# Key pieces in six places and an earlier mask in the first layer, pairs of heads in the second layer's attention

## The chip, the cores and the metric

One Trainium2 chip, one core of it. The time is the device time of one execution in microseconds (us), from the first to the last instruction of the program with what lies around it. Lower is better.

## What is computed

Two layers, each of cross attention to a long context, a mixing or attention block and a feed-forward block, with layer norms and residual sums. The work of all six blocks runs in one program. The two blocks that the change touches, with the shapes of this case (2 sequences of 256 tokens, 256 features, a context of 4096):

```python
# first layer, cross attention: 16 heads of 16
q = proj(layernorm(x), Wq, bq); k = proj(ctx, Wk, bk); v = proj(ctx, Wv, bv)
energy = einsum('bhqd,bhkd->bhqk', q, k) / sqrt(16)
energy = where(mask == 0, -1e9, energy)
x = x + softmax(energy) @ v @ Wo.T + bo

# second layer, attention: 16 heads of 64, heads 0-7 causal, heads 8-15 not
q, k = rope(h @ Wq), rope(h @ Wk); v = h @ Wv        # h = layernorm(x)
out_ar   = attend(q[:, :8], k[:, :8], v[:, :8], causal)
out_diff = attend(q[:, 8:], k[:, 8:], v[:, 8:], 0)    # softmax(q k^T / 8 + mask) v
x = x + concat(out_ar, out_diff) @ Wo
```

All is float32 at the interfaces. No key is masked in the inputs, and the kernel finds this out while it runs.

## The kernel before

**Engines and order.** The program is written by hand for each engine: one list of instructions for SP (DMA issues), ScalarE (`act`), VectorE (`dve`), TensorE (`pe`) and GpSimd (`pool`). Each list runs in its order; what ties them together are semaphores that are waited for by value. So the order of two instructions of one engine is that of the source, and one that waits holds up all behind it.

**First layer, up to the first exponentials.** The context of 4096 positions is cut in 8 chunks of 512 (`NCH`), each loaded as 512 KB into one of six slots (`SLOTS`). For each chunk `project_keys` makes two pieces of keys (128 of the 256 features each, four matmul records of 512 columns a piece) and `project_values` two halves of the values (eight records of 256 columns a half). Results go through a ring of three PSUM banks, which ScalarE empties (`copy_keys`, lines 692 and 693; `copy_values`, line 698). Keys and queries are kept as three bfloat16 parts that add up to the float32 value: ScalarE writes the high part and a float32 copy (`K32`, three buffers), VectorE subtracts and casts the middle part (`split_keys`, lines 975 and 977; `split_queries`, lines 961 to 968), and GpSimd subtracts the low part (`low_part`, line 607). A finished piece (`KPT`, three places, number of the piece modulo 3) is stored to DRAM (`store_k`, line 432) and read back in another arrangement as a stack of 96 rows (`load_stack`, six DMAs a quarter, line 440; `QST` for the queries, line 469). A place can be written again when its store has landed.

Meanwhile the mask (int32, four loads of 1 MB on ScalarE's queue, line 661) is turned into bfloat16 on VectorE in eight parts (`mask_part`, line 984), ScalarE sums each part (`sum_mask`, line 683), TensorE adds over partitions (line 1654), VectorE makes a flag (lines 1079 and 1081), and TensorE reads it and branches into `attend(True)` or `attend(False)`; in the latter no matmul adds the mask. `BRANCH` chunks are projected ahead of the branch. In `attend`, what is left of keys and values is interleaved with `scores`, 32 units of 128 queries by 1024 keys (two matmul records of 96 rows, line 1528), each followed by its row maximum on VectorE (`row_tops`, line 991). `LAG` says how many chunks the values stand behind the keys, `UNITS_AT` how many units go with each chunk. After that `turn_max` brings the maxima of the group into the stack, and the long loop over 8 groups of 4 heads starts, in which TensorE makes turned scores (line 1557), ScalarE takes exponentials (line 715) and TensorE weighs the values (line 1575).

**SP's list around it.** Stores of pieces, then, by chunk, the loads of the query stack, of the key stacks' quarters, and of context chunks 6 and 7 into the slots of chunks 0 and 1 when their values are made (line 445).

**Second layer's attention.** After rotation (`f_roped`), queries and keys are turned on TensorE and copied by ScalarE (line 886) so that even heads lie in partitions 0 to 63 and odd heads in 64 to 127. There are 32 units n of one sequence and head, 16 pairs. For each n: `head_scores` (two matmuls, four records, line 1921) into one of four PSUM banks; `row_maxima` on VectorE (for causal heads with the mask added and written to a buffer `PM`, line 1376; else a plain maximum, line 1381; then a negated, scaled copy, line 1383); `head_exps` on ScalarE (line 895); `scale_exps` on VectorE (a reciprocal, line 1389, and two multiplications of 128 rows of queries each, line 1393); `turn_weights` on TensorE (three or four transposes, line 1935, into bank 2 or 3); a copy of these by ScalarE (line 915); and for each pair `weigh_heads` on TensorE (eight records, the two heads to the two halves of the output partitions, line 1952) and `copy_contexts` on VectorE (line 1401). TensorE's loop takes scores of n + 3, turning of n, and after every odd n the weighing of the pair before. The values are projected ahead of the loop (line 1889).

## Time and profile before

| | us |
|---|---|
| median of 3 runs | 1050.47 |
| lowest and highest | 1048.58, 1052.31 |
| profiled execution | 1047.13 |
| its span, first to last instruction | 1045.3 |

| engine | busy us in the span | share |
|---|---|---|
| TensorE (PE) | 916.5 | 88% |
| VectorE (DVE) | 601.9 | 58% |
| ScalarE (ACT) | 487.4 | 47% |
| GpSimd (POOL) | 78.2 | 7% |

The mean granted TensorE clock over the span is 0.951 of full speed. How to read the rows below: times are in us from the span's start unless marked ns. PE is TensorE's matmuls and PEld its weight loads, which overlap; SPq and ACTq are DMA issues of these engines; L12 is line 12 of the kernel. A float32 matmul shows as two records. The chain of waits follows the work that ended last back to the start: at each step to what released it, or to the instruction before it on its engine; "issue" there is time in which the engine waited for nothing that the profile shows.

### The profile page before, as it was taken

The page shows a single profiled execution, that of the slowest core. Times are in us where ns is not written, and L with a number is a line of the kernel's source. Part 1 is how long each engine was busy: PE and PEld are TensorE (multiplying, and loading weights), DVE is VectorE, ACT ScalarE, POOL GpSimd, SP SyncE. Part 2 cuts the span into 40 slices and gives each one's busy share as a digit, 9 for nine tenths or more (in the row PEclk, how much of TensorE's full clock was granted, in tenths as well). Part 3 has the DMA queues.
Part 4 walks back from the last instruction along what each step waited for, and adds up shares of the span by engine and source line. Part 5 has one row for each costly group of instructions (what it writes and reads, how often), then busy time and mean ns, then how long its engine had stood idle before and what let it go on. Part 6 is the DMA issues. An engine that isn't in the chain of part 4 may idle for free.

```text
span 1045.3 us, 14987 instructions
## 1 busy us (share of the span) xinstructions
PE 916.5 (88%) x5913; PEld 527.1 (50%) x5914; DVE 601.9 (58%) x1064; ACT 487.4 (47%) x955; POOL 78.2 (7%) x87
## 2 busy tenths in 40 slices
PE   6379799999999999999988995059999989999878
PEld 2246444444555555555445543034755854566656
DVE  3647777777874458888443836953233127288240
ACT  1623366777764567777884411322220210677201
POOL 2312011111000000000002000300000007000000
PEclk9979899999999999999998998669999989999979
DMA  9845733454322212226028006032625350000000
GB/s 357 220 90 158 250 104 104 139 151 132 87 69 65 61 32 67 74 74 195 15 103 296 1 1 241 0 149 93 241 81 211 112 161 0 1 1 1 1 0 21
DMA packets 65555, 108.67 MB, mean 104 GB/s; under 512 B 6854, under 2 KB 40390, under 8 KB 63302
## 3 DMA queue, kind: packets, MB, share of 16 engines
q1 hardware_dynamic: 63276, 100.35, 30.3%
q10 hardware_dynamic: 2208, 7.34, 1.8%
q8 instruction: 49, 0.80, 0.3%
q14 instruction: 22, 0.18, 0.1%
HBM read 93.77 MB, written 13.89 MB: 103 GB/s over the span
## 4 chain that ended last, share of the span: by engine, by line
PE 79%; DVE 9%; ACT 6%; issue 3%; DMA 2%; SPq 0%; POOL 0%; ACTq 0%; DVEq 0%
PE psum L1575 12%; PE psum L1557 10%; PE psum L1528 10%; PE psum L1512 5%; PE psum L1860 5%; PE psum L1831 5%; PE psum L1502 5%; PE psum L1684 4%; PE psum L1889 4%; PE psum L1697 4%; PE psum L1921 3%; ACT arena L715 2%; PE psum L1935 2%; DVE arena L991 1%; PE psum L2021 1%
## 5 line engine op out<-in xcount | busy, mean ns | idle before, releaser
L991 DVE TENSOR_REDUCE arena<-psum 128x1 f32<-128x1024 f32 x256 | 301.7, 1219 | 121.2 <-PE psum L1528 121.1
L715 ACT ACTIVATE arena<-psum 128x512 f32<-128x512 f32 x512 | 264.7, 604 | 63.6 <-PE psum L1557 62.5
L1557 PE MATMUL psum<-arena 99*128 99x256 bf16 x1024 | 161.3, 275 | 8.4 <-ACT arena L715 4.8
L1528 PE MATMUL psum<-arena 96*128 96x512 bf16 x512 | 152.9, 382 | 6.5 <-DVE arena L991 5.5
L1575 PE MATMUL psum<-arena 128*32 128x256 f32 x2048 | 136.8, 385 | 0.0
L1557 PEld LDWEIGHTS psum<-arena 99*128 99x128 bf16 x1024 | 80.4, 98 | 107.1 <-ACT arena L715 50.6
L1575 PEld LDWEIGHTS psum<-arena 128*32 128x32 f32 x2048 | 53.5, 109 | 75.4 <-ACT arena L715 36.9
L1502 PE MATMUL psum<-arena 128*128 128x512 f32 x128 | 64.3, 630 | 24.1 <-DMA arena<-wkT 9.0
L1512 PE MATMUL psum<-arena 128*128 128x256 f32 x256 | 62.9, 389 | 1.3 <-ACT arena L693 1.3
L1528 PEld LDWEIGHTS psum<-arena 96*128 96x128 bf16 x512 | 49.4, 99 | 25.9 <-DVE arena L991 12.9
L607 POOL TENSOR_TENSOR arena<-arena 128x512 bf16<-128x512 f32 x34 | 40.8, 1199 | 213.4 <-DVE arena L977 206.7
L1512 PEld LDWEIGHTS psum<-arena 128*128 128x128 f32 x256 | 47.8, 192 | 16.7 <-issue 9.6
L1860 PE MATMUL psum<-arena 128*128 128x256 f32 x256 | 55.9, 379 | 0.0
L1831 PE MATMUL psum<-arena 128*128 128x512 f32 x128 | 55.5, 593 | 0.0
L692 ACT ACTIVATE arena<-psum,arena 128x512 bf16<-128x512 f32 x32 | 22.0, 686 | 67.0 <-PE psum L1502 50.3
L1860 PEld LDWEIGHTS psum<-arena 128*128 128x128 f32 x256 | 48.3, 190 | 6.4
L1502 PEld LDWEIGHTS psum<-arena 128*128 128x128 f32 x128 | 24.4, 200 | 49.7 <-issue 39.2
L1684 PE MATMUL psum<-arena 128*128 128x512 f32 (+1 forms) x112 | 44.1, 551 | 3.3 <-ACT arena L781 0.9
L698 ACT ACTIVATE arena<-psum 128x512 f32<-128x512 f32 x32 | 19.1, 597 | 59.7 <-PE psum L1512 59.7
L877 ACT ACTIVATE arena<-psum 128x512 f32<-128x512 f32 x16 | 9.6, 597 | 78.5 <-PE psum L1847 78.5
L1889 PE MATMUL psum<-arena 128*128 128x512 f32 x96 | 43.2, 610 | 0.7 <-ACT arena L779 0.7
L1303 DVE CUSTOM_DVE_ANT_0 arena<-psum,arena 128x512 f32<-128x512 f32 x32 | 22.1, 692 | 32.9 <-PE psum L1831 30.7
(234 smaller groups left out, 989.0 us busy)
## 6 DMA issues: line engine op xcount, KB each, us to landing
arena<-kparts SPq DMA_DIRECT2D x192, 128.0 KB, 3.1
kparts<-arena SPq DMA_DIRECT2D x32, 384.0 KB, 3.4
arena<-ctxT SPq DMA_DIRECT2D x18, 512.0 KB, 5.1
arena<-ctxT SPq DMA_DIRECT2D x2, 4096.0 KB, 12.9
arena<-ctx SPq DMA_DIRECT2D x2, 4096.0 KB, 14.3
arena<-mask SPq DMA_DIRECT2D x8, 1024.0 KB, 6.8
arena<-mask ACTq DMA_DIRECT2D x4, 1024.0 KB, 12.2
arena<-w1e SPq DMA_DIRECT2D x2, 2048.0 KB, 10.2
```

The lines of the kernel that those rows point to most:

```text
L715: nc.scalar.activation(PR[step % 4][:, pair * CH:(pair + 1) * CH], ring_bank(slot), ACT.Exp)\
L991: nc.vector.tensor_reduce(MX[g % 2][:, col:col + 1], unit_banks(n).rearrange("p b n -> p (b n)"), AX.X, ALU.max).then_inc(s_maxed, 1)
L1502: last = nc.tensor.matmul(ring_bank(slot), WK[:, k, f * P:(f + 1) * P], CTX[n % SLOTS][:, k, :], start=(k == 0), stop=(k == CT - 1))
L1512: last = nc.tensor.matmul(ring_bank(slot)[:, v * 256:(v + 1) * 256], CTX[n % SLOTS][:, k, (2 * i + v) * P:(2 * i + v + 1) * P], WV[:, k, : ...
L1528: last = nc.tensor.matmul(out, q, KST[g % 2][0:ROWS, j, at], start=True, stop=not masked, skip_group_check=True)
L1557: last = nc.tensor.matmul(ring_heads(slot)[:, u, :], KST[gg % 2][0:KROWS, j, kc * P:(kc + 1) * P], QST[0:KROWS, G * g + j, b * S:(b + 1) * S],
L1575: last = nc.tensor.matmul(PV[32 * j:32 * (j + 1), :], V_flat[:, at:at + 32], PR[step % 4][:, j * S:(j + 1) * S], start=(kc == 0), stop=(kc ...
L1684: last = nc.tensor.matmul(out, weights[:, k, m * P:m * P + width], xs[k], start=(k == 0), stop=(k == n - 1))
L1697: last = nc.tensor.matmul(out, lhs[k], weights[:, k, :], start=(k == 0 and not biased), stop=(k == n - 1), skip_group_check=biased)
L1831: last = nc.tensor.matmul(psum[:, n % 4, :], QC[:, c, w * P:(w + 1) * P], CTXT[w // 2][:, c, n * 512:(n + 1) * 512], start=(c == 0), stop= ...
L1860: last = nc.tensor.matmul(psum[:, 6, 0:256], PT1[:, k * P:(k + 1) * P], CTXK[w // 2][:, k, :], start=(k == 0), stop=(k == KC - 1))
L1889: last = nc.tensor.matmul(psum[:, bank, :], HTF[:, c, i * P:(i + 1) * P], WQKV[which][:, c, half * HALF:(half + 1) * HALF], start=(c == 0) ...
```

## The change

What it does, in the first layer:

- `KPT` has six places (`PLACES`) up to the last piece of the first sequence and three after it. ScalarE no longer waits for the store three pieces back but for that six pieces back, and besides for the low part three pieces back (the float32 buffers stay three). `piece_number`, `place` and `turn_at` do the counting; the queries' pieces come after two chunks (`EARLY = 2`).
- Masks are loaded after chunks 0 and 1 (of which 1 comes behind masks 0 and 1), the other chunks after all of them. VectorE makes mask parts 0 to 3 after chunk 0 and 4 to 7 after chunk 1, then splits the queries, then waits for the count. ScalarE sums four parts after the keys of chunk 1 and four after those of chunk 2, in place.
- TensorE projects chunk 1 ahead of the queries and chunk 2 behind them, then branches: `BRANCH` 3 instead of 4. `LAG` is 4 instead of 3, so no values are made ahead of the branch; `UNITS_AT` gives 4 units to each of steps 4 to 11, where it was 4 to each of 4 to 9 and 8 to step 10. In `attend` the wait for the query stack stands ahead of the first unit, and each half step has keys, values, two units. The loads of context 6 and 7 stand one chunk later on SP, context 6 behind the second stack.
- The copy of the turned x and the first splits change order on VectorE; a few small loads share semaphores.

In the second layer's attention:

- `head_scores` takes a pair: for each half of the queries the even head and then the odd head. TensorE's loop runs over pairs: scores of the pair two ahead, turning of both heads, weighing of the pair before.
- The factor -1/8 is in ScalarE's copy of the turned queries, so the maximum becomes a minimum and the negated copy is gone.
- `scale_exps` multiplies the second 128 queries on VectorE and GpSimd the first 128.
- Even heads' turned weights are copied by VectorE (`copy_weights`, bank 2), odd ones by ScalarE (bank 3). The values' projection uses four banks instead of five.

```diff
-LAG = 3
-BRANCH = 4
+LAG = 4
+BRANCH = 3
+EARLY = 2
+PLACES = 6
 AHEAD = 6
 RAMP = 5
-UNITS_AT = {4: 4, 5: 4, 6: 4, 7: 4, 8: 4, 9: 4, 10: 8}
+UNITS_AT = {4: 4, 5: 4, 6: 4, 7: 4, 8: 4, 9: 4, 10: 4, 11: 4}
...
-        KPT = [b16(45584 + 768 * i, 1536).rearrange("p (r n) -> p r n", r=3) for i in range(3)]
+        KPT = [b16(at, 1536).rearrange("p (r n) -> p r n", r=3) for at in (45584, 46352, 47120, 41488, 42256, 43024)]
...
         def piece_number(b, c, f):
 
-            return f if b + c == 0 else CT + 2 * NCH * b + 2 * c + f
+            return 2 * NCH * b + 2 * c + f + (CT if b or c >= EARLY else 0)
 
         def query_piece(f):
-            return CT + f
+            return 2 * EARLY + f
+
+        def place(r):
+
+            first = CT + 2 * NCH
+            return r % PLACES if r < first else (r - first) % 3
+
+        def turn_at(r):
+
+            return sum(place(n) == place(r) for n in range(r + 1))
...
+            def chunks_stored(first):
+                for c in (first, first + 1):
+                    for f in range(CT):
+                        stored(piece_number(0, c, f))
+
+            for c in range(EARLY):
+                for f in range(CT):
+                    store_k(0, c, f)
             for f in range(CT):
                 r = query_piece(f)
                 sp.wait_ge(k_low, r + 1)
+                sp.dma_start(qparts[:, f * P:(f + 1) * P, :].rearrange("r p n -> p r n"), KPT[place(r)])\
+                  .then_inc(k_stored[place(r)], 16)
+            sp.dma_start(arena[ROWS:KROWS, 0:8192], t["ones"]).then_inc(q_stacked, 16)
+            chunks_stored(0)
+            load_stack(0, 0)
+            for f in range(CT):
+                stored(query_piece(f))
+            for r in range(6):
+                sp.dma_start(QST[r:ROWS:6, :, :], qparts[Q_PARTS[r]].rearrange("(h d) n -> d h n", d=DH))\
+                  .then_inc(q_stacked, 16)
+            for c in range(EARLY, NCH):
                 for f in range(CT):
                     store_k(0, c, f)
                 if c == 3:
                     sp.wait_ge(mask_step, 8)
+                    sp.dma_start(arena[ROWS:KROWS, 8192:16384], t["ones"]).then_inc(late_loaded, 16)
+                    sp.dma_start(BV, t["rows"][:, ROW_AT["bv"]:ROW_AT["bv"] + 256].broadcast_to((P, 256)))\
+                      .then_inc(late_loaded, 16)
+                    sp.dma_start(AW, t["A"].rearrange("(t p) s -> p t s", p=P)).then_inc(on["bm_loaded"], 16)
+                if c == 4:
+                    chunks_stored(2)
+                    load_stack(0, 1)
                     first_values_done(0)
                     load_ctx(0, 6, 0)
+                if c == 5:
                     first_values_done(1)
                     load_ctx(0, 7, 0)
                 if c == 6:
+                    chunks_stored(4)
                     load_stack(0, 2)
+            chunks_stored(6)
...
             for idx in range(4 * NCH):
                 pool.wait_ge(k_split, 2 * (idx + 1))
-                low_part(idx if idx < CT else idx + CT)
-                if idx == CT - 1:
+                low_part(idx if idx < CT * EARLY else idx + CT)
+                if idx == CT * EARLY - 1:
                     for f in range(CT):
                         pool.wait_ge(q_split, 4 * (f + 1))
...
-            pool.wait_ge(on["f_roped"], 16)
+            for n in range(32):
+                pool.wait_ge(on["f_inverse"], n + 1)
+                part = PM[n % 4][:, 0, 0:keys(n, 0)]
+                nc.gpsimd.tensor_scalar(part, part, FRI[:, 2 * n:2 * n + 1], None, ALU.mult)\
+                  .then_inc(on["f_scaled_p"], 1)
+
...
-            for c in range(3):
-                load_ctx(c)
+            load_ctx(0)
             load_mask(0)
             load_mask(1)
+            load_ctx(1)
             act.wait_ge(built, 3)
             nc.scalar.activation(TABLES[:, 0:1], ONES[:, 0:1], ACT.Sqrt)
             act.wait_ge(ln_var, 1)
             nc.scalar.activation(SD[:, 0:4], SD[:, 4:8], ACT.Sqrt).then_inc(ln_sd, 1)
-            load_ctx(3)
             load_mask(2)
             load_mask(3)
-            for c in range(4, SLOTS):
+            for c in range(2, SLOTS):
                 load_ctx(c)
 
             def sum_mask(i):
                 qt, half = i // 4, i % 4
                 act.wait_ge(mask_step, i + 1)
-                if i >= 4:
-                    act.wait_ge(mask_summed, i - 3)
                 at = slice(half * 2 * CH, (half + 1) * 2 * CH)
-                nc.scalar.activation(UNREAD[i % 4], MASKB[:, qt, at], ACT.Copy, accum_out=MSUM[:, i:i + 1])\
+                nc.scalar.activation(MASKB[:, qt, at], MASKB[:, qt, at], ACT.Copy, accum_out=MSUM[:, i:i + 1])\
                   .then_inc(mask_summed, 1)
 
             def copy_keys(b, c, f):
                 slot, r = KEY_AT[b, c, f], piece_number(b, c, f)
                 act.wait_ge(ring_filled, slot + 1)
+                if turn_at(r) > 1:
+                    act.wait_ge(k_stored[place(r)], 16 * (turn_at(r) - 1))
                 if r >= 3:
-                    act.wait_ge(k_stored[r % 3], 16 * (r // 3))
+                    act.wait_ge(k_low, r - 2)
                 bias = COLT[:, COL_AT["bk"] + f:COL_AT["bk"] + f + 1]
-                nc.scalar.activation(KPT[r % 3][:, 0, :], ring_bank(slot), ACT.Identity, bias=bias).then_inc(k_copied, 1)
+                nc.scalar.activation(KPT[place(r)][:, 0, :], ring_bank(slot), ACT.Identity, bias=bias).then_inc(k_copied, 1)
...
+                if 0 < c < BRANCH:
+                    for part in range(4 * (c - 1), 4 * c):
+                        sum_mask(part)
...
+                if n < 8:
+                    signal(nc.scalar.activation(QT[:, n, :], psum[:, n, :], ACT.Copy, scale=-(DM ** -0.5)),
+                           "f_turned_copied")
+                else:
+                    signal(nc.scalar.activation(KT[:, n - 8, :], psum[:, n - 8, :], ACT.Copy), "f_turned_copied")
...
-            for n in range(32):
-                if n + 2 < 32:
+            for pair in range(16):
+                n = 2 * pair + 1
+                if pair + 1 < 16:
+                    head_exps(n + 1)
                     head_exps(n + 2)
                 act.wait_ge(on["f_pt"], n + 1)
-
-                if n >= 4:
-                    act.wait_ge(on["f_pv"], (n - 4) // 2 + 1)
+                if pair >= 2:
+                    act.wait_ge(on["f_pv"], pair - 1)
                 width = keys(n, 0) + keys(n, 1)
-                signal(nc.scalar.activation(PTM[n % 4][:, 0:width], psum[:, 2 + n % 2, 0:width], ACT.Copy),
-                       "f_pt_copied")
+                signal(nc.scalar.activation(PTM[n % 4][:, 0:width], psum[:, 3, 0:width], ACT.Copy), "f_pt_copied_a")
...
+                        copy_turned_x()
+                    if c < BRANCH - 1:
+                        for i in range(4):
+                            mask_part(4 * c + i)
+                    if c == EARLY - 1:
                         for f in range(CT):
                             split_queries(f)
-                    if c in (1, 2):
-                        for i in range(4):
-                            mask_part(4 * (c - 1) + i)
-                    if c == BRANCH - 1:
                         dve.wait_ge(mask_counted, 1)
                         nc.vector.tensor_reduce(FLAGF[0:1, 0:1], psum[0:1, 3, 0:8], AX.X, ALU.min).then_inc(mask_step, 1)
                         dve.wait_ge(mask_step, 9)
...
+                        nc.vector.tensor_tensor_reduce(PM[n % 4][:, qt, 0:seen], src[:, qt, 0:seen],
+                                                       causal[:, qt, 0:seen], 1.0, 3.0e38, ALU.add, ALU.min,
+                                                       FMX[:, 2 * n + qt:2 * n + qt + 1]).then_inc(on["f_bias"], 1)
                 else:
+                    nc.vector.tensor_reduce(FMX[:, 2 * n:2 * n + 2], src, AX.X, ALU.min).then_inc(on["f_bias"], 2)
 
             def scale_exps(n):
                 dve.wait_ge(on["f_exp"], 2 * (n + 1))
+                nc.vector.reciprocal(FRI[:, 2 * n:2 * n + 2], FSUM[:, 2 * n:2 * n + 2]).then_inc(on["f_inverse"], 1)
+                dve.wait_ge(on["f_inverse"], n + 1)
+                part = PM[n % 4][:, 1, :]
+                nc.vector.tensor_scalar(part, part, FRI[:, 2 * n + 1:2 * n + 2], None, ALU.mult)\
+                  .then_inc(on["f_scaled"], 1)
+
+            def copy_weights(n):
+                dve.wait_ge(on["f_pt"], n + 1)
+                if n >= 4:
+                    dve.wait_ge(on["f_pv"], n // 2 - 1)
+                width = keys(n, 0) + keys(n, 1)
+                nc.vector.tensor_copy(PTM[n % 4][:, 0:width], psum[:, 2, 0:width]).then_inc(on["f_pt_copied_v"], 1)
...
-            for n in range(3):
+            for n in range(4):
                 row_maxima(n)
-            scale_exps(0)
-            for n in range(32):
-                if n + 1 < 32:
-                    scale_exps(n + 1)
-                if n + 3 < 32:
-                    row_maxima(n + 3)
-                if n % 2 == 0 and n > 2:
-                    copy_contexts((n - 4) // 2)
+            for n in range(2):
+                scale_exps(n)
+            for pair in range(16):
+                n = 2 * pair
+                if pair >= 2:
+                    copy_contexts(pair - 2)
+                for ahead in (n + 4, n + 5):
+                    if ahead < 32:
+                        row_maxima(ahead)
+                if pair + 1 < 16:
+                    scale_exps(n + 2)
+                copy_weights(n)
+                if pair + 1 < 16:
+                    scale_exps(n + 3)
...
             def attend(masked):
-                pe.wait_ge(q_stacked, 96)
                 n = 0
                 for c in range(BRANCH, NCH + LAG):
                     for i in range(2):
                         if c < NCH:
                             project_keys(0, c, i)
-                            scores(n, masked)
-                            n += 1
-                        project_values(0, c - LAG, i)
-                        for _ in range(UNITS_AT[c] // 2 - (c < NCH)):
+                        if c >= LAG:
+                            project_values(0, c - LAG, i)
+                        for _ in range(UNITS_AT.get(c, 0) // 2):
+                            if n == 0:
+                                pe.wait_ge(q_stacked, 112)
                             scores(n, masked)
                             n += 1
...
-            pe.wait_ge(wq_loaded, 16)
+            for f in range(CT):
+                project_keys(0, 1, f)
+            pe.wait_ge(wqv_loaded, 32)
             pe.wait_ge(ht_ready, CT)
             for f in range(CT):
                 for c in range(CT):
                     last = nc.tensor.matmul(psum[:, f, :], WQ[:, c, f * P:(f + 1) * P], HT[:, c, :],
                                             start=(c == 0), stop=(c == CT - 1))
                 last.then_inc(q_psum, 1)
-            pe.wait_ge(wv_loaded, 16)
-            for c in range(1, BRANCH):
-                for i in range(2):
-                    project_keys(0, c, i)
-                    if c >= LAG:
-                        project_values(0, c - LAG, i)
+            for f in range(CT):
+                project_keys(0, 2, f)
...
+            def head_scores(pair):
+
+                if pair >= 2:
+                    pe.wait_ge(on["f_exp"], 4 * (pair - 1))
                 for qt in range(2):
+                    for n in (2 * pair, 2 * pair + 1):
+                        b, h, p0, k = unit(n)
+                        last = nc.tensor.matmul(HEAD_SCORES[n % 4][:, qt * S:qt * S + keys(n, qt)],
+                                                QT[p0:p0 + DM, k, b * S + qt * P:b * S + (qt + 1) * P],
+                                                KT[p0:p0 + DM, k, b * S:b * S + keys(n, qt)], start=True, stop=True)
+                        if qt:
+                            last.then_inc(on["f_scores"], 1)
 
             def turn_weights(n):
+                pe.wait_ge(on["f_scaled"], n + 1)
+                pe.wait_ge(on["f_scaled_p"], n + 1)
                 if n >= 2:
+                    pe.wait_ge(on["f_pt_copied_a" if n % 2 else "f_pt_copied_v"], n // 2)
...
+            for pair in range(16):
+                if pair + 2 < 16:
+                    head_scores(pair + 2)
+                turn_weights(2 * pair)
+                turn_weights(2 * pair + 1)
+                if pair:
+                    weigh_heads(pair - 1)
```

## Rows read from the trace of the kernel before

**Rows 1.** Stretches: length; busy us of PE, PEld, DVE, ACT, POOL; granted clock; DMA.

```profile
50.00:75.00 25.00, 16.25 (x50) 9.68 (x51) 8.93 (x12) 5.67 (x11) 2.87 (x3) 0.70 0.40 97
911.31:966.15 54.84, 54.84 (x323) 34.43 (x324) 44.85 (x192) 42.09 (x145) 0.00 (x0) 1.00 0.00 1
```

**Rows 2.** Chain of waits, 0 to 140 us: start, length, what.

```profile
23.81 7.58 DMA qparts<-arena
...
51.72 7.59 issue
59.31 3.75 PE psum L1502 x4
...
66.72 1.72 PE psum L1502 x4
68.44 0.43 PE psum L1528 x2
...
114.91 4.63 DVE arena L991 x4
```

**Rows 3.** Instructions in order of time, 0 to 64 us: start, length, engine, line.

```profile
16.80 0.68 DVE L975 TENSOR_TENSOR arena<-arena 128x512 f32<-128x512 f32 x1
...
18.03 1.53 POOL L607 TENSOR_TENSOR arena<-arena 128x512 bf16<-128x512 f32 x1 [15.05 <-DVE arena L977]
...
18.58 1.26 DVE L977 CAST arena<-arena 128x512 bf16<-128x512 f32 x1
...
26.46 0.75 DVE L961 TENSOR_SCALAR arena<-psum,arena 128x512 f32<-128x512 f32 x1 [3.91 <-DMA kparts<-arena]
...
33.08 0.69 ACT L692 ACTIVATE arena<-psum,arena 128x512 bf16<-128x512 f32 x1 [0.34 <-DMA qparts<-arena]
...
40.58 3.46 DVE L984 TENSOR_SCALAR arena<-arena 128x1024 bf16<-128x1024 int32 x4
...
48.44 1.06 ACT L683 ACTIVATE arena<-arena 128x1024 bf16<-128x1024 bf16 x1
```

**Rows 4.** DMA issued between 9.7 and 10.2 us: size, us to landing.

```profile
arena<-mask ACTq DMA_DIRECT2D x1, 1024.0 KB, 13.4
```

**Rows 5.** DMA issued between 76.7 and 77.2 us (context chunk 7).

```profile
arena<-ctxT SPq DMA_DIRECT2D x1, 512.0 KB, 5.8
```

**Rows 6.** The eight context loads of line 445 up to 130 us.

```profile
DMA to landing us min/median/max: 4.3/6.4/8.3
```

**Rows 7.** Chain of waits, second layer's attention: causal pairs, full pairs, the end.

```profile
914.88 0.48 PE psum L1935 x3
915.36 0.85 PE psum L1921 x4
...
916.68 0.80 PE psum L1952 x8
...
926.67 1.06 PE psum L1921 x4
927.73 0.59 PE psum L1935 x4
...
932.40 1.01 PE psum L1952 x8
...
969.19 1.90 PE psum L1952 x16
```

**Rows 8.** VectorE's groups by shape, 911.3 to 966.1: busy, mean ns.

```profile
L1393 DVE TENSOR_SCALAR arena<-arena 128x256 f32<-128x256 f32 x42 | 13.5, 349 | 0.5
L1381 DVE TENSOR_REDUCE arena<-psum 128x2 f32<-128x512 f32 x16 | 11.0, 688 | 4.9 <-PE psum L1921 4.9
L1376 DVE CUSTOM_DVE_ANT_0 arena<-psum,arena 128x256 f32<-128x256 f32 x13 | 5.5, 420 | 0.0
...
L1389 DVE RECIPROCAL arena<-arena 128x2 f32<-128x2 f32 x28 | 4.4, 157 | 0.0
```

**Rows 9.** GpSimd's groups by shape, whole span.

```profile
L630 POOL TENSOR_SCALAR arena<-arena 128x16 f32<-128x16 f32 x16 | 4.8, 324 | 0.1
```

155 lines of the change are left out of this document (43 added, 112 removed).

## Prediction

> **What bounds the kernel now.** I read the table of stretches first. In 50 to 75 us TensorE works 16.25 of 25 us at a mean granted clock of 0.70; in 911.31 to 966.15 us, the loop of the second layer's attention, it works all 54.84 us at clock 1.00 beside VectorE with 44.85 and ScalarE with 42.09 [rows 1]. So the first edit meets a stage with idle TensorE, the second a stage that TensorE fills. Then the chain of waits. In the first stage it runs through a wait of 7.58 us for the store of a query piece to land (one of three places for split pieces must come free), through mask counting, and through 7.59 us of "issue" after the flag is computed, in which TensorE reads the flag and jumps into `attend`; the first matmul there starts at 59.31 [rows 2]. From there TensorE is the chain until VectorE's row maxima take over; the last four end at 119.54 [rows 2]. In the second stage the chain is TensorE alone: for a causal pair of heads 2 x (0.85 scores + 0.48 turning) + 0.80 weighing = 3.46 us, for a full pair 2 x (1.06 + 0.59) + 1.01 = 4.31 [rows 7].
>
> **First stage, up to `attend`.** The edit removes ScalarE's and VectorE's waits for stores (six places), sends masks 2 and 3 behind two chunks instead of four, and enters `attend` after three chunks, not four. What is late next is VectorE's own queue, in its new order. Its splits of chunk 0 and the copies of the turned x end by 19.84 as before, only reordered [rows 3]. Then mask parts 0 to 3, 3.46, to 23.3; two splits of chunk 1, which now as before collide with GpSimd (16.80 to 19.84, 3.04), to 26.3; mask parts 4 to 7, 3.46, to 29.8 [rows 3]. Their data is there: the last mask load, issued at about 9.8, took 13.4 us, landing near 23, and now 1 MB less is ahead of it [rows 4]. First query split: 0.75 and three more of at most 0.75, 2.4 to 32.2; GpSimd's low part without collision, about 1.2, to 33.4. ScalarE's copy of the last piece of chunk 2 now waits for that low part (it frees the float32 buffer): two copies of 0.69, to 34.8; behind it stand the last four mask sums at 1.06, to 39.0 [rows 3]. Count and flag took 1.1 us (sum of 48.44's row plus three more ends near 50.6, the "issue" starts at 51.72), then 7.59: `attend` at 47.7, 11.6 us sooner [rows 2, 3]. The second query split and its low part end near 36; SP then issues that store and the twelve loads of stacks behind it; the first scores, near 57, leave them 21 us. The branch I keep at 7.59; its bounds are 0 and twice that, since no other branch is in the trace, and nothing in the edit touches it.
>
> **What that start gives back.** `attend` now has chunk 3 to project: 2 x 1.72 = 3.4. TensorE comes out of its pause slowly as before: the same four matmuls took 3.75 at 59.31 and 1.72 at 66.72 [rows 2]; that is the lower level, 1.2 GHz, and the mean of 0.70 in that stretch [rows 1]. In all 2.9 us are lost, as before. Chunk 4 thus starts at 47.7 + 3.4 + 2.9 = 54.0. Half a chunk is keys 1.72, values 1.72 (eight records of half the columns), two units 0.86: 4.31. Chunk 6 would start at 54.0 + 17.2 = 71.2. But its context goes into the slot of chunk 0, whose values are now made in chunk 4, and its load is queued on SP behind chunk 4's stores and the six loads of a stack. In the trace the load in that very place in the queue (chunk 7's) is issued at 76.7 and takes 5.8 [rows 5]; the second half of chunk 4 began at 66.6, so it lands 20.3 us after a chunk 4 at full clock: 74.3. **A new stall of 3.1 us**; with landings of 4.3 to 8.3 [rows 6] it is 1.6 to 5.6. Then two chunks, 17.2, and four chunks of values and units, 8 x 2.6 = 20.9 : 112.4. The last maxima end 2.1 us later, at 114.5; the burst of eight units in one chunk, 4.63 us per four on VectorE [rows 2], is gone. 119.5 - 114.5 = **5.0 us** gained; 8 without the stall, 2 with a branch or stall some us longer.
>
> **Second stage, TensorE.** Scores of a pair alternate between partitions 0 to 63 and 64 to 127. No such pair is in the trace. The nearest row is the weighing, whose two heads go to the two halves of the columns: eight records in 1.01 us including its start, when four records of one head's scores alone take 1.06 [rows 7]. So two halves of the array do work side by side there, and I take a pair of scores at one head's price, 1.06 (full) and 0.85 (causal). Bounds: this, and no overlap, where only the fixed 0.21 of the second head goes. Turning both heads in one go saves one fixed part: 4 records take 0.59 and 3 take 0.48, so 0.15 is fixed [rows 7]: 1.03 and 0.81. Pair: full 1.06 + 1.03 + 1.01 = 3.10, causal 0.85 + 0.81 + 0.80 = 2.46.
>
> **Second stage, the others.** ScalarE loses half of its copies and stays under TensorE. VectorE loses 32 small negations and half of the scaling, and takes 16 copies of 512 columns. Per full pair: 2 maxima at 0.69, 2 reciprocals at 0.16, 2 scalings at 0.35, a copy at 0.69 (the price of a 512-column maximum from PSUM), a context copy at 0.42 (256 columns): 3.5 by durations [rows 8]. Its instructions overlap: four maxima of the first layer end 1.16 apart with a duration of 1.22 [rows 2], so 8 x 0.06 comes off: 3.05. So TensorE and VectorE are level, and I take **3.2** with what their handshakes leave. The new wait is the one for GpSimd, which scales the first 128 query rows: TensorE's turning, with weighing and the next scores queued behind it, waits for that. The price of that instruction is not in the trace: 128 x 16 takes 0.32 [rows 9], a two-input 128 x 512 takes 1.15 to 1.53 [rows 3]; I take 0.5 to 0.6, near the lower since it has one input and a quarter to half of the columns. For causal heads the maxima write into the buffer that turning must have left, so a loop closes: maximum 0.6, scaling of the other head 0.45, copy 0.5, reciprocal 0.2, VectorE's scaling 0.3, GpSimd 0.5, turning 0.35, three handoffs of 0.1: **3.2** per causal pair, not 2.46. From the first weighing to the end of the last the trace shows 916.68 to 971.09, 54.4 us [rows 7]; now fourteen periods of 3.2 plus two weighings, 44.8 + 1.9 = 46.7, with a first weighing at the same place: 7.7, and some tenths from the pause before 969: **8 us**.
>
> The VectorE scaling and GpSimd's start on the same reciprocal. In the trace a VectorE cast of 0.43 took 1.26 while GpSimd ran from 18.03 to 19.56 [rows 3]: each waits for the other. The Trainium skill agrees (GPSIMD Engine Reference, the table at the top): their SBUF interfaces are shared, with contention for two-port modes. By its "TensorEngine Tiling (Array Packing)", Performance Considerations, row tiles run in parallel but the emptying of PSUM does not speed up and may become the bottleneck; the trace shows no row tiles. By its first half alone the loop would follow TensorE's 2.46 and 3.10; by its second half it is what I forecast.
>
> **Sum.** The profiled execution took 1047.13 with a span of 1045.3; the median of the three runs is 1050.47, 3.3 higher. 1047.1 - 5.0 - 8 = 1034, and with the 3.3 put back, **1037**.
>
> **Rivals.**
> (a) Row halves do not run side by side. Full 1.9 + 1.03 + 1.01 = 3.95, causal at its loop, 3.2: 7.5 x 3.95 + 6.5 x 3.2 = 50.4 instead of 44.8; gain 5 + 2.5, **1043**. For it: nothing in the trace shows row halves. Against: column halves do.
> (b) The first stage gives nothing, because VectorE's longer queue ahead of the flag, or context 6, costs 5 us more than I have: **1042**. For it: the landing row reaches 8.3.
> (c) No loop but TensorE counts in the second stage, and context 6 lands early: 6.5 x 2.46 + 7.5 x 3.10 = 39.2, gain 13.6 + 8: **1029**.
> (d) Slower: the exchange between VectorE and GpSimd. If GpSimd's instruction costs 1.15 and VectorE loses 0.83 once per pair, the loop is 3.2 + 0.65 + 0.83 = 4.7 for every pair; 14 x 4.7 instead of 52.5 (54.4 - 1.9) is 13 us lost, less 5: **1058**. It decides from a mean period of 4.1 us. Against it: 32 rows of GpSimd work at 1.15 or more have twice the inputs and columns.
> (e) (a) and (b) together, or half of (d): within 3 us of before, **1048**.
>
> **Chances.** Forecast 0.46 (own range 1033 to 1041), (a) 0.14, (b) 0.12, (c) 0.12, (d) 0.09, (e) 0.07. The range 1029 to 1045 leaves out (d), (e) and little else. Faster by over 0.3% (about what a measurement of this kernel can tell, 3 us) 0.84; within 0.07; slower 0.09.
>
> **What would show it.** Right: first matmul of `attend` near 48; no wait for kparts or qparts on ScalarE or VectorE; TensorE waits 2 to 5 us for ctxT at chunk 6; last maximum of the first 32 near 114.5; pair period 3.1 to 3.4 with VectorE near full; eight score records in about 1.06; last weighing about 13 us sooner than 971. Wrong: score records of a pair that take 1.9; GpSimd rows over 0.8; VectorE scalings well over 0.35; a flag computed after 42.

## The result, and the profile of the changed kernel

The changed kernel takes 1034.05 us in the median of four runs (1030.18 to 1035.36), the kernel before 1051.39 beside it (1048.58 to 1053.05): a ratio of 0.984, 95% interval 0.981 to 0.988. It is **faster by 1.6%**. The profiled execution took 1030.18 us with a span of 1028.4, against 1047.13 and 1045.3 before. Measured once more, in six runs, the changed kernel took 1035.21 (0.986, 0.983 to 0.989).

First the chain of waits up to the first scores. Columns: start, length, what; an x counts records. It answers to [rows 2].

```profile
1.75 10.66 DMA arena<-wkT
12.46 6.44 PE psum L1522 x8
...
23.15 1.89 DVE arena L999 x3
...
27.93 3.45 DVE arena L999 x4
...
38.17 2.28 ACT arena L693 x5
...
41.53 6.22 issue
47.74 7.55 PE psum L1522 x12
```

The 7.58 us in which the chain waited for a query piece's store are gone. The flag is there at 41.53 instead of 51.72, and `attend` begins at 47.74 instead of 59.31. But the first matmul now waits for the key weights until 12.4 us. Next TensorE's own rows, with the idle time before each and what ended it in brackets.

```profile
69.79 1.03 PE L1548 MATMUL psum<-arena 96*128 96x512 bf16 x4
73.29 1.98 PE L1522 MATMUL psum<-arena 128*128 128x512 f32 x4 [2.47 <-DMA arena<-ctxT]
...
917.26 1.13 PE L1940 MATMUL psum<-arena 64*128 64x256 f32 x8
918.32 1.25 PE L1955 MATMUL psum<-arena 128*128 128x128 f32 x8
919.51 1.08 PE L1973 MATMUL psum<-arena 128*64 128x256 f32 x8
920.52 0.93 PE L1940 MATMUL psum<-arena 64*128 64x128 f32 x8
...
923.76 0.93 PE L1940 MATMUL psum<-arena 64*128 64x128 f32 x8
924.97 0.63 PE L1955 MATMUL psum<-arena 128*128 128x128 f32 x4 [0.28 <-POOL arena L657]
```

At 73.29 the keys of chunk 6 wait 2.47 us for their context: a stall that the kernel before did not have. The last of the first 32 row maxima ends at 113.9, 5.6 us sooner than the 119.54 of [rows 2]. Behind it stands one turn of the second layer's loop, with eight score records, eight turnings and eight weighings: 3.26 us from scores to scores without a gap in TensorE's rows. Eight score records of 64 rows take about 1.1 us, the time of four in [rows 7]. The next turn takes 3.24, from 920.52 to 923.76.

The table of stretches of the same kernel, three pairs whose scores are full, and the whole loop; after it the waits of that loop by engine and line (total, times, longest). They answer to [rows 1].

```profile
core 0: us, PE busy (x) PEld busy (x) DVE busy (x) ACT busy (x) POOL busy (x), PEclk, DMA share, GB/s
907.80:917.33 9.53, 8.85 (x71) 5.61 (x70) 9.28 (x27) 6.87 (x28) 5.68 (x7) 1.00 0.01 3
901.77:953.08 51.31, 45.68 (x352) 28.19 (x352) 44.08 (x155) 36.80 (x137) 27.78 (x32) 1.00 0.00 1
```

```profile
POOL arena L657 <- DVE arena L1398: 31.5, 21, 13.2
DVE arena L1390 <- PE psum L1955: 14.6, 8, 12.3
...
PE psum L1955 <- POOL arena L657: 2.0, 3, 1.2
```

The loop ends 51.31 us after its start instead of 59.78 (its old window ended at 971.09 [rows 7]): **8.5 us**. VectorE is busy 9.28 of 9.53 us, more than TensorE. It looks like the bound; an experiment below shows that taking work off it does not shorten the stretch. By this table GpSimd waits for VectorE's reciprocals far longer than anyone waits for GpSimd. The table understates the second: of TensorE's 5.6 us of idle time ahead of turnings it puts 2.0 down to GpSimd and most of the rest to "issue", but every one of these stretches ends 0.10 to 0.28 us after GpSimd's scaling for that head has ended (see "Is VectorE the bound of the pair?").

**Where the 16.9 us of the two spans lie.** I followed the start of the same matmul in both traces. 5.6 us are gained by the first row maxima, 6.1 inside the last group of heads of the first attention (515.4), and still 6.1 at the first matmul behind that attention (552.6). The next stretch, untouched, gives 2.8: 12.82 us in place of 15.66. The code from there to the second attention gives 0.6 more, that attention 8.5, and the tail after it loses 1.1. So 14.6 us come from the edit and 2.3 from stretches that it doesn't touch; of these the last section treats the 2.8.

### The profile page after: what moved, and what is told of

It is laid out like the page before. It is cut to its first block, busy times and chain, and to the rows that moved or that the text cites. A ratio compares the mean times of both kernels' runs of the same rounds, so it can differ in the third digit from the quotient of the medians.

```text
span 1028.4 us, 14977 instructions
## 1 busy us (share of the span) xinstructions
PE 898.5 (87%) x5914; PEld 517.0 (50%) x5914; DVE 596.5 (58%) x1016; ACT 478.1 (46%) x939; POOL 106.7 (10%) x119
## 4 chain that ended last, share of the span: by engine, by line
PE 78%; DVE 10%; ACT 6%; issue 3%; DMA 2%; POOL 1%; SPq 0%; ACTq 0%; DVEq 0%
PE psum L1595 12%; PE psum L1577 10%; PE psum L1548 9%; PE psum L1878 5%; PE psum L1849 5%; PE psum L1522 5%; PE psum L1532 5%; PE psum L1702 4%; PE psum L1907 4%; PE psum L1715 4%; ACT arena L727 2%; PE psum L1955 2%; PE psum L2043 1%; PE psum L1940 1%; DVE arena L1006 1%
## 6 DMA issues: line engine op xcount, KB each, us to landing
arena<-w1e SPq DMA_DIRECT2D x2, 2048.0 KB, 10.2
```

## The experiments

All were timed in turn with the kernel before on the same chip. The ratio is to that kernel, with its 95% interval. "Maxima" is the end of the first layer's first 32 row maxima: 119.5 before, 113.9 changed, but 117.8 in the second profile of the changed kernel. "Second" is the distance in one profile from the first matmul of the second attention's query projection to the first of the router behind that attention (133.35 before, 125.38 changed).

**One part alone.** The edit splits cleanly into its two stages.

```
first_alone:  six places, masks, three chunks, values four behind; second layer as before
second_alone: heads in pairs, GpSimd's scaling; first layer as before
```

> Only the first layer's part of the change (six places, earlier mask, branch after three chunks, values four chunks behind); the second layer's attention is that of before. Theory: the gain of this part is what its own stage shows in the changed kernel, attend's first matmul at 47.7 instead of 59.3, the last of the first 32 maxima at 113.9 instead of 119.5, so 5 to 6 us less than before, about 1045.5. Rival (the part is worth more, since the whole program lies 9.5 us earlier when the second attention starts): 9 to 10 us less, with the 3.4 us between 510 and 800 us coming from the edit. If instead those 3.4 us are the granted clock in a stage that the change does not touch (0.75 and 0.91 in 555 to 575 of before, 1.00 in the changed one), they come and go from execution to execution and the mean stays at 5 to 6.

> Only the second layer's part (pairs of heads, GpSimd scaling one half, copies shared). Theory: the stretch from the values' last copy to the end of the last weighing takes 51.3 us as in the changed kernel instead of 59.8, so 8.5 us less than before, about 1042.5; the first part and this one add up to the whole. Rival (they do not add up, because part of the whole's 17 us is clock): this one and the other together give less than 15 us.

| kernel | us | ratio | maxima | second |
|---|---|---|---|---|
| first part | 1041.44 | 0.992 (0.988 to 0.996) | 117.3 | 133.3 |
| second part | 1041.41 | 0.992 (0.989 to 0.994) | 120.6 | 125.4 |

Each gives some 9 us against the 1050.54 beside them, and within their intervals (some 3 to 4 us either way) they add up: 18 of 17.3. For the first part the 9.1 us are the rival's figure, not the 5 to 6 of my theory, but its interval reaches from 4 to 13 us, so the medians do not settle it. In its profile the stretch behind the first attention, which the edit doesn't touch, ran in 12.8 us, as in the changed kernel, where the kernel before had 15.7; that is 2.8 us of the 5.9 by which the two spans differ. In the profile of the second part "second" is 7.9 us shorter; of the first part's, only 2.2 us show at the maxima. Its `attend` began at 47.8 as in the changed kernel and its stall was 2.9; what it lost came behind that, as the table of stretches of this kernel shows:

```profile
60.00:75.00 15.00, 12.09 (x45) 7.29 (x44) 11.03 (x13) 5.37 (x9) 3.46 (x3) 0.93 0.76 208
75.00:90.00 15.00, 15.00 (x49) 9.09 (x48) 8.12 (x11) 5.59 (x9) 2.37 (x3) 0.85 0.30 95
```

The granted clock was 0.93 and 0.85 of full; the changed kernel had 1.00 in both. The same code thus yields maxima between 113.9 and 117.8 (113.0 in a kernel below that differs only in the second layer), and no verdict on a few us of the first stage can rest on this mark alone. I use the starts ahead of it.

**What makes two heads cost the price of one?** My first guess was the alternation: a matmul of one head, then one of the other.

```diff
-                for qt in range(2):
-                    for n in (2 * pair, 2 * pair + 1):
+                for n in (2 * pair, 2 * pair + 1):
+                    for qt in range(2):
```

> The changed kernel with one thing undone: within a pair, both score matmuls of the even head come before both of the odd head. Theory (the row halves of the array work side by side only when neighbouring matmuls go to different halves): eight records of a full pair take 1.9 us instead of 1.06, the period of full pairs goes from 3.2 to about 3.9 and TensorE is the bound there, while causal pairs stay at their loop of 3.2; 5 to 6 us more than the changed kernel, about 1040. Rival (the gain of the stage is VectorE's lighter load and the turning of two heads in one go, the halves do not matter): within 1 us of the changed kernel, about 1034.

1037.07 us, 0.986 (0.982 to 0.991), second 125.5. TensorE's rows for one pair:

```profile
924.94 1.14 PE L1940 MATMUL psum<-arena 64*128 64x256 f32 x8
926.01 1.25 PE L1955 MATMUL psum<-arena 128*128 128x128 f32 x8
```

The eight records take what they took before, though all four of the even head now stand ahead of the odd head's. The median lies between the 1040 of the theory and the 1034 of the rival and settles nothing; the rows do. **The alternation fell** as a reason. What was left was that the heads are neighbours at all; the next kernel parts them.

```diff
-                    head_scores(pair + 2)
+                    head_scores(pair + 2, (0,))
                 turn_weights(2 * pair)
+                if pair + 2 < 16:
+                    head_scores(pair + 2, (1,))
                 turn_weights(2 * pair + 1)
```

> The changed kernel, but in the second layer's loop the turning of the even head's weights stands between the even head's two score matmuls and the odd head's two. The same matmuls, other neighbours. Theory: what the pair gains is that a head's 64 rows run beside the other head's 64 rows, for which the two heads must be neighbours on TensorE; then the scores of a pair cost 2.12 us again in place of 1.06 (full) and 1.7 in place of 0.86 (causal). With TensorE busy 8.85 of 9.53 us in three full pairs that is 0.8 us a pair more after the slack is used, over 14 pairs 8 to 11 us: the loop from first to last matmul some 134 us by the marks that give 125.4 with the change and 133.35 before, the kernel 1042 to 1045. Rival: the gain came from fewer or better placed waits and from the exchange with GpSimd; then the order costs within 2 us and four records of one head still take about 0.53 each way.

1045.93 us, 0.9965 (0.994 to 0.999). This is 3.1 us under the kernel before, where the three other kernels timed beside it are 13 to 16 under: most of the gain is gone, by one change of order. One pair, TensorE:

```profile
923.67 1.13 PE L1940 MATMUL psum<-arena 64*128 64x256 f32 x4
...
926.12 1.13 PE L1940 MATMUL psum<-arena 64*128 64x256 f32 x4
...
927.76 1.13 PE L1940 MATMUL psum<-arena 64*128 64x256 f32 x4
```

Four records of one head take the 1.13 that eight took above, and a pair takes 4.09 us (923.67 to 927.76) where it took 3.26. From the first weighing to the router it takes 75.1 us in place of 66.4: 8.7 more, inside the 8 to 11 expected, and as much as the old order's 74.2 (in first_alone). This is shown: the second layer's gain is two heads in the two row halves at once. It does not need the alternation, only that the two heads' matmuls follow each other without the turning between them.

**What is GpSimd's half of the scaling worth?** All of it on VectorE:

```diff
-                pool.wait_ge(on["f_inverse"], n + 1)
-                nc.gpsimd.tensor_scalar(part, part, FRI[:, 2 * n:2 * n + 1], None, ALU.mult)\
...
+                for qt in range(2):
+                    part = PM[n % 4][:, qt, 0:keys(n, qt)]
+                    nc.vector.tensor_scalar(part, part, FRI[:, 2 * n + qt:2 * n + qt + 1], None, ALU.mult)\
```

> The changed kernel with both halves of the scaling on VectorE, as before, and none on GpSimd. Theory (VectorE's time is the bound of the loop; it was busy 9.28 of 9.53 us in a steady stretch): two more scalings a pair at 0.27 (causal 0.2) us between starts, so 16 times about 0.5, 7 to 8 us more than the changed kernel, about 1041. Rival (what holds the pair's period at 3.2 is the wait for GpSimd's 0.76 and 1.06 us): the relief of that wait pays for the longer list, within 2 us of the changed kernel or faster.

1037.40 us, 0.987 (0.983 to 0.992), second 127.98: **2.6 us** more, much nearer to the rival's end. Turning now waits for VectorE's scaling where it waited for GpSimd, in total and times:

```profile
PEld psum L1950 <- DVE arena L1397: 15.9, 29, 1.7
...
PE psum L1950 <- DVE arena L1405: 6.7, 14, 1.4
```

VectorE is then busy 48.9 of 54.4 us, so it was not full even there.

**Is VectorE the bound of the pair?** Its 16 context copies go to ScalarE.

```diff
+                act.wait_ge(on["f_pv"], pair + 1)
+                signal(nc.scalar.activation(OT[:, k, b * S:(b + 1) * S], psum[:, 4 + pair % 2, 0:S], ACT.Copy),
+                       "f_pv_copied")
...
-                nc.vector.tensor_copy(OT[:, k, b * S:(b + 1) * S], psum[:, 4 + pair % 2, 0:S])\
-                  .then_inc(on["f_pv_copied"], 1)
```

> The changed kernel, with the 16 copies of a pair's contexts out of PSUM in the second layer's attention on ScalarE in place of VectorE (6.2 us of VectorE's 44.1 in a loop of 51.3; ScalarE has 36.8). Theory: VectorE (9.28 busy of 9.53 in three full pairs) is level with TensorE (8.85), so that taking 0.42 a pair from it brings the full pairs from 3.2 to TensorE's 3.0 and no further: 1 to 3 us less. Rival: the pair is bound by the chain from exponentials to turning, so that VectorE's work is beside the point or ScalarE's extra 0.4 a pair delays the exponentials: no change, or 1 to 3 us slower.

1035.95 us, 0.989 (0.987 to 0.992). The stretch of three full pairs, by engine:

```profile
912.84:922.37 9.53, 8.80 (x70) 5.73 (x72) 8.81 (x25) 7.79 (x32) 6.14 (x8) 1.00 0.01 2
```

VectorE fell from 9.28 to 8.81 us and the three pairs still take 9.53; from the first weighing to the router it is 66.2 us in place of 66.4. So the rival was right: VectorE's sum of work was not what held the pairs. In the turn with eight turnings shown further up, TensorE's rows are full, 3.26 us without a gap. Where causal heads are turned they have a gap of up to 0.37 us, which the profile calls "issue", and the turns take 2.9 to 3.4 us. Here are rows of all three engines around one such gap in the changed kernel, in order of time:

```profile
932.81 0.52 PE L1955 MATMUL psum<-arena 128*128 128x128 f32 x3 [0.36 <-issue]
933.47 0.29 DVE L1390 CUSTOM_DVE_ANT_0 arena<-psum,arena 128x128 f32<-128x128 f32 x1 [0.24 <-PE psum L1955]
934.06 1.13 PE L1940 MATMUL psum<-arena 64*128 64x256 f32 x8
934.97 0.15 DVE L1398 RECIPROCAL arena<-arena 128x2 f32<-128x2 f32 x1
935.20 0.52 PE L1955 MATMUL psum<-arena 128*128 128x128 f32 x3
935.21 0.76 POOL L657 TENSOR_SCALAR arena<-arena 128x128 f32<-128x128 f32 x1 [0.16 <-DVE arena L1398]
936.08 0.52 PE L1955 MATMUL psum<-arena 128*128 128x128 f32 x3 [0.36 <-issue]
937.33 1.13 PE L1940 MATMUL psum<-arena 64*128 64x256 f32 x8
```

The gap is a wait for GpSimd. Its scaling for the odd head ends at 935.98, and that head's turning starts at 936.08. In every pair from the second to the fifteenth, of causal and of full heads, the odd head's turning starts 0.10 us after its scaling on GpSimd has ended, also where TensorE's rows show no gap. For causal heads the loop can be read off: turning of the odd head (932.81), then the maximum (now taken as a minimum) that writes into the buffer it has left (933.47), VectorE's list up to the odd head's reciprocal (934.97), GpSimd (935.21 to 935.98), the next odd turning (936.08): 3.27 us. The context copy that this experiment moved stands behind that reciprocal in VectorE's list, so it is outside the loop. With the copies on ScalarE the odd turning still starts 0.10 to 0.22 us after GpSimd's end in each of these pairs. What sets GpSimd's start for full heads I did not follow, and no run shortened GpSimd's instruction alone.

**The stall at chunk 6.** Its load goes ahead of the stack in SyncE's queue.

```diff
                 if c == 4:
+                    first_values_done(0)
+                    load_ctx(0, 6, 0)
                     chunks_stored(2)
                     load_stack(0, 1)
-                    first_values_done(0)
-                    load_ctx(0, 6, 0)
```

> The changed kernel, with the load of context chunk 6 ahead of the stack that SyncE waits for in the same turn. Theory: the stall of 2.5 us at the first key matmul of chunk 6 (TensorE waiting for the load) is only this queue order; the load starts earlier, the stall goes, and the last of the first 32 row maxima ends 2.5 us sooner, with the whole kernel 1 to 2.5 us faster. Rival: the load is then not late, but the stack is, and its user stalls in its place: no change within 1 us; or the row maxima on VectorE were the bound there, and TensorE gives it back.

1032.89 us, 0.986 (0.984 to 0.988). No wait for the context is left, nothing waits for the stack instead, and the maxima end at 111.8, 2.1 sooner than 113.9, which alone would lie within that mark's spread. The missing wait shows it: the stall was the queue order. By its time alone the kernel can't be told from the changed one.

**TensorE's pause as room for more.** A fourth chunk of keys ahead of the branch:

```diff
-BRANCH = 3
+BRANCH = 4
...
-            for f in range(CT):
-                project_keys(0, 2, f)
+            for c in (2, 3):
+                for f in range(CT):
+                    project_keys(0, c, f)
```

> The changed kernel with one more chunk of keys projected ahead of the branch (four chunks in place of three). Theory: TensorE's pause before and in the branch (6.2 us that end with the branch taken, after about 5 us of waits for the mask) takes the 3.4 us of projection without the attention starting later, and the last of the first 32 maxima ends up to 3.4 us sooner; the kernel 1 to 3.4 us faster. Rival: the 6 us of the branch follow the end of TensorE's last matmul ahead of it, whatever the flag's time, so that the branch is left 3.4 us later and nothing is gained; or the context of chunk 6 is then later by just as much, its stall 5.9 in place of 2.5.

1034.73 us, 0.986 (0.983 to 0.989). TensorE in this kernel:

```profile
40.53 0.57 PE L1673 MATMUL psum<-arena 128*128 128x8 f32 x2 [7.09 <-ACT arena L693]
47.90 3.75 PE L1522 MATMUL psum<-arena 128*128 128x512 f32 x4 [6.81 <-issue]
...
55.02 1.04 PE L1548 MATMUL psum<-arena 96*128 96x512 bf16 x4 [1.39 <-DMA arena<-qparts]
...
72.16 3.49 PE L1522 MATMUL psum<-arena 128*128 128x512 f32 x4 [3.18 <-DMA arena<-ctxT]
```

The branch is left at 47.9 as before, so the extra 3.4 us of projection did fit into the pause; but the first scores then wait for the query rows until 55.02, the stall at chunk 6 is 3.18, its first four matmul records take 3.49 us at a granted clock of 0.54 (the lower level, 1.2 GHz, is 0.50) in place of 1.98, and the maxima end at 114.5. Nothing is gained. Neither of my two accounts named the query rows.

**No branch at all.** The flag is still computed, but TensorE reads none and runs the unmasked half; the masked half is left out.

```diff
-            any_masked = pe.value_load(FLAG, min_val=0, max_val=1)
-            with pe.If(any_masked == 1):
-                attend(True)
-            with pe.Else():
-                attend(False)
+            attend(False)
```

> The changed kernel with the flag and the branch left out: TensorE goes straight into the unmasked attention, which is the half that this data takes, and the masked half is left out. Theory: the 6 us in the branch and the wait for the flag ahead of it are no longer the bound, but the query rows, which land at 55 us (with four chunks ahead the first scores waited for them until 55.0, against 56.9 with the change), stand right behind; so the first scores come 1.9 us sooner and the last maxima 1 to 2 us sooner, kernel 1032 to 1034. Rival: with 15 us more for TensorE ahead of the scores, keys and values of chunks 3 and 4 are done in advance and the last maxima end 4 to 6 us sooner.

1034.82 us, 0.985 (0.981 to 0.989). TensorE:

```profile
41.80 7.35 PE L1522 MATMUL psum<-arena 128*128 128x512 f32 x12 [0.42 <-DVE arena L1097]
...
55.09 1.06 PE L1548 MATMUL psum<-arena 96*128 96x512 bf16 x4 [4.21 <-DMA arena<-qparts]
```

`attend` starts 5.9 us sooner, 0.05 us after the flag is computed (at 41.75) and 0.42 after TensorE's matmul that counts the masks; the 5.9 us are the price of reading the flag and jumping. Of it 4.2 us go to the same wait for the query rows, so the first scores come at 55.1 in place of 56.9. Behind that the clock was at 0.93 and 0.84 as in the first part's profile, with maxima at 117.7. Against the changed kernel on the same chip (1035.21) it gives 0.4 us, which is nothing. **Taking the branch away alone gains little**: 1.8 us reach the first scores, because the query rows stand right behind it, and in this profile the lower clock took them back.

**What six places are worth.** Three places in the new order:

```diff
-PLACES = 6
+PLACES = 3
...
+                dve.wait_ge(k_stored[place(r)], 16 * (turn_at(r) - 1))
```

> The changed kernel with three places for the split keys in place of six, the order of everything else left as changed. Theory: in the new order the query pieces and chunk 3's keys reuse a place while its store is still under way (stores are issued from 20.2 us on and take 4 to 8 us), so ScalarE and VectorE wait and the branch is left some 3 to 8 us later; kernel 1037 to 1041. Rival: the earlier masks do the work alone and the places are worth less than 1 us.

1041.43 us, 0.992 (0.989 to 0.995), 6.2 over the changed kernel beside it. The chain shows where:

```profile
22.01 4.35 issue
26.36 0.69 ACT arena L704
...
38.52 1.15 DMA qparts<-arena
39.67 4.15 ACT arena L693 x8
```

ScalarE's copy of a key piece waits for its place until 26.36 (the store of the first piece lands at 26.29), and the last mask sums stand behind another copy (at 38.40) that waited 3.8 us for a query piece's store; `attend` begins at 52.2, 4.5 us later than with six places. So of the first stage's 11.6 us ahead of `attend` at least 4.5 are the places.

**The key weights.** Both loads moved: chunk 6 as above, and ScalarE issues all four mask loads from 8.4 us on, none ahead of the key weights.

```diff
             load_ctx(0)
-            load_mask(0)
-            load_mask(1)
             load_ctx(1)
...
-            load_mask(2)
-            load_mask(3)
+            for i in range(4):
+                load_mask(i)
```

> The changed kernel with chunk 6's context load ahead of the stack, as in ctx6_first, and all four mask loads issued where the last two of them were (after ScalarE's first square root, at 8.4 us), so that none lies ahead of the key weights. Theory: the key weights landed at 12.4 in place of 9.0 us because 2 MB of masks were queued beside them; they land near 9 again, the first key matmul starts 3.4 us sooner, and the branch is left between 44.3 and 46 in place of 47.7, if the masks still land before their turn on VectorE (19 to 20 us). The last of the first 32 maxima then ends at 108.5 to 111 in place of 113.9 (111.9 with the context load alone); kernel 1028 to 1031. Rival: the masks now land after VectorE is ready for them, at 20 us or later, and the flag is no earlier than 41.5: nothing beyond what the context load gives.

> The changed kernel once more, unaltered. Expected 1034, ratio 0.984 to 0.987. In the profile the stretch between the first matmuls of the two feed-forward parts of the first layer, which the change does not touch, took 12.8 us once and 15.7 us in the other kernels with this or the old second layer. If the two values come by run and not by kernel, it takes 12.8 or 15.7 here, either way, with a granted clock of 1.00 or below 0.95 in it; if this kernel's earlier arrival brings the faster one, it takes 12.8 again.

Two loads moved: 1030.40 us (1028.70 to 1032.08), 0.981 (0.977 to 0.984). The changed kernel beside it: 1035.21 (1033.64 to 1038.92). The ranges don't touch, though the intervals of the two ratios do (0.977 to 0.984, 0.983 to 0.989): **4.8 us faster than the changed kernel in the median, 20 faster than the one before**. Its chain:

```profile
19.77 2.41 DVE arena L997 x4
...
38.65 6.17 issue
44.83 8.39 PE psum L1520 x12
```

and TensorE's first row:

```profile
8.66 6.00 PE L1520 MATMUL psum<-arena 128*128 128x512 f32 x8 [8.66 <-DMA arena<-wkT]
```

The weights are there at 8.66 in place of 12.4. The masks, issued from 8.4 us on, land between 13.5 and 21.0: the first two before VectorE comes to them at 19.77, the last two before their turn at 25.05. Every later step to the branch is 2.9 us sooner. Maxima: 109.1, 4.8 sooner; 2.9 of it is this start, and the other 1.9 is about what the context load gave in the run above.

## The prediction, step by step

**`attend` at 47.7: right to 0.1 us, by three errors that cancel, which is luck.** The key weights came 3.4 us later than I let them, because I moved the mask loads only through VectorE's queue and not past the key weights in the queues of transfers (two masks issued at 1.25 and 1.80 us, the weights at 1.75); two_loads shows that this was the cause. With it VectorE's first mask part started at 22.55, not 19.84. Against that, mask parts 0 to 3 took 2.49, not 3.46. The four parts 4 to 7 did take 3.45, but not evenly: three of them lasted 0.68 as the first four did, and one, which started at 28.53 while GpSimd's low part ran from 28.08 to 29.62, lasted 1.64. And "issue" took 6.22, not 7.59. In all I had the flag at 40.1 and it came at 41.5. The step that failed was "splits of chunk 0 end by 19.84 as before": it took a start as given that the edit's own DMA order moved.

**The stall at chunk 6: 3.1 forecast, 2.5 measured**, in a range of 1.6 to 5.6; mechanism and place are shown by ctx6_first. **Maxima: 114.5 forecast, 113.9 measured**; but a second profile of the same code has 117.8, since I took the slow coming out of the pause as 2.9 us always, and there the granted clock was down again behind it (0.83 of full from 75 to 90 us, 1.00 in the first profile). That 113.9 came so near is in part luck; the term should have had a spread of 4 us.

**Scores of a pair at one head's price: right.** It rested on rows of column halves and was the weakest-founded term; scores_apart shows it is worth 8.7 us, which makes rival (a) the one that was closest to mattering. Turning eight took 1.19, not 1.03: that is twice the 0.59 of [rows 7], so one fixed part of 0.15 was not saved by putting the heads together, and a turn of the loop with them is 3.26, not 3.10.

**GpSimd at 0.5 to 0.6: wrong by half.** Its instruction takes 0.76 on 128 columns and 1.06 on 256 (mean 0.92 of 30). I had leaned to the low end because it has one input; the row it lay nearest to was the two-input one at 1.15. 1.06 is beyond the 0.8 that I had named as a sign of being wrong. The forecast survived it, but not because GpSimd is done ahead of need: nearly all of TensorE's 5.6 us of idle time in the loop ends about 0.1 us after a scaling on GpSimd, as shown above. What a shorter instruction would give no run shows. Rival (d) had that price nearly right and its other half wrong: VectorE's scalings kept 0.35 beside GpSimd, with no 0.83 lost. The lengthening that I had read from the cast came for casts (1.27 at 26.74) and for that one mask part.

**The causal loop of 3.2: right, with terms that are off both ways.** It measures 3.27 where it can be read off. GpSimd took 0.76 in it, not 0.5; against that VectorE's own scaling, 0.3, is not on its path, since GpSimd starts on the reciprocal. From the second pair's odd turning to the last one's the fourteen periods take 44.1 us, 3.15 each.

**VectorE level with TensorE: the number right, the reason not shown.** 9.28 busy of 9.53, 3.1 a pair by my sum; but taking 0.47 us from it changed nothing. In the turn of eight turnings whose rows are full TensorE alone needs 3.26; my 3.10 for it made VectorE's 3.05 look level.

**Second stage 8 us: 8.5 measured. Sum:** in profiled terms 1034 against 1030.2, of which 2.3 us are the untouched stretches and the rest is 0.6 and 0.5 in the two stages and 0.5 between the maxima and the last group of the first attention; in medians 1037 against 1034. The last weighing ends 18.0 us sooner than 971, not 13, and 3.4 of the 5 us between are those of the stretches ahead of it that the edit doesn't touch. The tail behind it gives 1.1 of them back. Rival (c), TensorE alone, would have had 2.46 for a causal pair; the shortest turn took 2.9. The Trainium skill's page "TensorEngine Tiling (Array Packing)" says in its Performance Considerations that tiling speeds up TensorE but not the emptying of PSUM; the traces agree with the first half (eight records in 1.13 us), and no run here tested the second.

## To carry to other kernels

When an edit reorders loads, follow the queue of every transfer from the first microsecond, not only the engine that waits: here 2 MB of masks issued beside 0.25 MB of weights made the first matmul 3.4 us late, and putting them behind, with one more load moved forward, gave 4.8 us. Matmuls of 64 rows from the two halves of the partitions are worth placing next to each other; other work between the two took the whole gain. An engine that is 97% busy is not thereby the bound: take 5% of its work away and see whether the period moves, and ask whether that work lay on the loop. And where the profile calls a gap "issue", list when each of the instructions it had to wait for ended: one that ends the same 0.10 us ahead of it every time is the likely one.

## What the runs showed of the hardware

**Row halves.** Two heads' matmuls run side by side even when all records of one stand in program order ahead of the other's: eight in 1.13 to 1.14 us either way, four of one head also in 1.13. I had thought that they must alternate.

**The granted clock differs in a stretch whose code is the same.** The second row of each table below starts at the first matmul behind the first attention; the first row is the 5 us ahead of it, in which TensorE's busy time is the same to 0.01 us in all profiles. Columns as above, TensorE only. The kernel before:

```profile
553.69:558.69 5.00, 4.16 (x59) 1.00 0.39 147
558.69:563.69 5.00, 4.41 (x17) 0.63 1.00 359
563.69:568.69 5.00, 4.91 (x16) 0.68 1.01 433
```

The changed kernel:

```profile
547.60:552.60 5.00, 4.15 (x59) 1.00 0.38 143
552.60:557.60 5.00, 4.26 (x23) 1.00 0.97 365
557.60:562.60 5.00, 4.33 (x44) 1.00 1.00 429
```

Of the clock's two levels, 1.00 is the upper, 2.4 GHz, and 0.50 would be the lower, 1.2 GHz; 0.63 and 0.68 are means over both. From the first matmul behind the attention to the first one with 512 columns behind it the same work takes 15.66 us in the first and 12.82 in the second. Of 14 profiles, three take 12.8 there (both of the changed kernel, and first_alone), three_places 14.5, and ten 15.6 to 15.7. It is not the time of arrival: the three begin it at 552.6, 556.4 and 556.9, and others at 553.0 and 556.35 have the lower clock. Both profiles of the changed kernel had it and no other kernel with its second layer did, so it may be this program's or chance; what decides it stays open. Together with the first stage's 4 us of spread this is more than an edit of 3 us is worth, so such an edit can't be read from the spans of two profiles; from the chain and the starts it can.

**A branch costs TensorE about 6 us.** From the flag's end to the next matmul the chains show 7.59 before and 8.58 in second_alone, 6.0 to 6.4 in eight kernels with six places, 7.3 in three_places; without the branch it is 0.05. Why it differs stays open.
